# One attention stage and a state-space scan: mask, summed states and sums of squares taken from other places

## The reference

```
# attention 1: 16 query heads, 4 key heads, 128 wide, causal
qkv = x @ w_qkv.T
q, k = layernorm(q) * g + b, layernorm(k) * g + b      # per head, over its 128 values
q, k = rope(q), rope(k)
scores = q @ k.T / sqrt(128);  scores = where(causal, -inf, scores)
out = softmax(scores) @ v @ w_o.T
# state-space layer 1: 256 channels, 16 states n, 4 batches
state[n] = state[n] * exp(delta * A[n]) + delta * u * B[n]     # along the positions
y = sum over n of state[n] * C[n]  + D * u
```

## Time and profile before

| | |
|---|---|
| median of 3 runs | 912.32 us |
| the profiled execution's own time | 913.75 us |
| its span, first to last instruction | 912.0 us |
| busy: PE, DVE, ACT, POOL | 767.7, 703.3, 445.6, 340.6 us |
| mean granted TensorE clock | 0.924 |

### The profile page before, as it was taken

How to read it: one execution, slowest core, us unless ns; L and a number is a source line. 1 busy time by engine, 2 the same in 40 slices (tenths; PEclk the granted TensorE clock), 3 DMA queues, 4 the chain that set the end, 5 groups by cost and what they waited for, 6 DMA issues and landing times.

```text
span 912.0 us, 12288 instructions
## 1 busy us (share of the span) xinstructions
PE 767.7 (84%) x3984; PEld 563.1 (62%) x3984; DVE 703.3 (77%) x1229; ACT 445.6 (49%) x928; POOL 340.6 (37%) x242
## 2 busy tenths in 40 slices
PE   6771459877798996799999999999955799999997
PEld 2241346554433563477767776777743689999996
DVE  4869779889857976999999999999977544444443
ACT  1663368650336402666566556756642354444442
POOL 1001346552330422233333323432343286666663
PEclk9785579998799998999999999999987899999999
DMA  4313223345020212011111211111300243334431
GB/s 171 121 47 114 93 94 125 115 139 218 1 98 0 74 43 92 19 40 44 51 36 36 69 36 36 55 39 36 118 0 1 79 158 138 138 138 138 141 135 46
DMA packets 28884, 74.63 MB, mean 82 GB/s; under 512 B 3633, under 2 KB 6337, under 8 KB 28449
## 3 DMA queue, kind: packets, MB, share of 16 engines
q1 hardware_dynamic: 28384, 71.51, 23.2%
q10 hardware_dynamic: 448, 2.49, 0.8%
HBM read 72.55 MB, written 1.44 MB: 81 GB/s over the span
## 4 chain that ended last, share of the span: by engine, by line
PE 50%; DVE 26%; issue 11%; ACT 9%; POOL 3%; DMA 1%; POOLq 0%; DVEq 0%; SPq 0%; ACTq 0%
PE ps L1671 6%; PE ps L1785 6%; PE ps L1786 6%; PE ps L1787 6%; PE ps L1631 4%; DVE hS L976 3%; PE ps L1651 3%; PE ps L1750 3%; PE ps L1435 2%; PE ps L1738 2%; DVE arena L1280 2%; DVE hS L1006 2%; DVE ps L968 2%; PE ps L1408 1%; PE ps L1720 1%
## 5 line engine op out<-in xcount | busy, mean ns | idle before, releaser
L403 POOL TENSOR_TENSOR hS<-hS,BCb 128x512 f32<-128x512 f32 x64 | 81.6, 1278 | 131.9 <-issue 66.7
L1387 DVE SCALAR_TENSOR_TENSOR arena<-ps,arena 128x1024 f32<-128x1024 f32 x32 | 39.2, 1224 | 102.2 <-ACT arena L842 93.1
L426 POOL TENSOR_TENSOR hS<-hS,BCb 128x1024 f32<-128x1024 f32 x23 | 56.1, 2440 | 111.3 <-DVE ps L968 96.3
L1671 PE MATMUL ps<-WB,hT 128*128 128x512 f32 x192 | 88.0, 603 | 3.0 <-DVE arena L1261 2.0
L476 POOL TENSOR_TENSOR MHl<-arena,MHh 128x1024 fp32r<-128x1024 f32 x34 | 81.7, 2404 | 16.9 <-ACT MHh L845 16.9
L1416 PE MATMUL ps<-ident,hS 128*128 128x128 f32 x256 | 40.1, 311 | 54.7 <-POOL hS L426 31.2
L1785 PE MATMUL ps<-Wh,MHh 128*128 128x256 f32 x272 | 77.8, 286 | 6.0 <-POOL MHl L476 6.0
L1006 DVE TENSOR_TENSOR_SCAN hS<-dA,ps 128x512 f32<-128x512 f32 x64 | 78.1, 1220 | 2.2
L1786 PE MATMUL ps<-Wl,MHh 128*128 128x256 f32 x272 | 77.6, 285 | 0.0
L1787 PE MATMUL ps<-Wh,MHl 128*128 128x256 f32 x272 | 77.5, 285 | 0.0
L1416 PEld LDWEIGHTS ps<-ident,hS 128*128 128x128 f32 x256 | 32.6, 159 | 65.1 <-POOL hS L426 38.2
(11 more groups left out here) (233 smaller groups left out, 1967.4 us busy)
## 6 DMA issues: line engine op xcount, KB each, us to landing
BCb<-bc_dram SPq DMA_DIRECT2D x32, 512.0 KB, 3.7
BCb<-bcq_dram SPq DMA_DIRECT2D x64, 256.0 KB, 3.1
arena<-gate_dram SPq DMA_DIRECT2D x32, 512.0 KB, 3.7
WB<-in_we SPq DMA_DIRECT2D x34, 256.0 KB, 2.7
WB<-in_wqkv SPq DMA_DIRECT2D x1, 3072.0 KB, 12.7
WA<-in_wo ACTq DMA_DIRECT2D x1, 2048.0 KB, 7.7
WA<-in_ffn SPq DMA_DIRECT2D x1, 1408.0 KB, 7.9
pkb<-in_pk SPq DMA_DIRECT2D x2, 698.0 KB, 4.7
```

What stands on the lines that cost most here:

```text
L403: gp.tensor_tensor(h, h, qbc(q)[:, 1:2, :].broadcast_to([P, DT, S]), ALU.mult).then_inc(s["c_ready"], 1)
L426: gp.tensor_tensor(h, h, BCb[g % SB_LOADS][:, 1:2, :].broadcast_to([P, DT, HALF]), ALU.mult).then_inc(s["c_ready"], 1)
L1671: last = mm(ps[:, bank + t, :], hT[:, c, P * (2 * b + t):P * (2 * b + t) + P], WB[:, c, c0:c0 + 512], start=(c == 0), stop=(c == HC - 1))
```

## The change

1. `s1` writes the mask only to the two diagonal blocks, 2 x 128 columns in place of 384.
2. `times_cq` of every odd step is followed on GpSimd by an addition of the even step's product, also 128 x 512, behind a wait for the product's own semaphore; `accq` is issued for odd steps only, so PE has half the transposes. The counts that the others wait for follow (`cq_count`, the ring's waits in `scanq` and `yq_copy`).
3. `job_sum` goes from VectorE. `job_sq` is eight ACTIVATEs of 128 x 128, one for each head and half of the positions, and each also gives the sum of its row through `accum_out`. GpSimd's part of the job waits for `job_sq`.
4. In the plan's table the price of "sum" goes, so steps of the scan move to other slots.

```diff
@@ -265,6 +265,7 @@
+        cq_count = lambda q: LAYER_STEPS + 3 * (q // 2) + q % 2 + 1
@@ -321,7 +322,7 @@
...
             def load_bq(q):
...
-                sp.wait_ge(s["c_ready"], LAYER_STEPS + max(q - QRING + 1, 0))
+                sp.wait_ge(s["c_ready"], cq_count(q - QRING) if q >= QRING else LAYER_STEPS)
@@ -401,6 +402,9 @@
...
             def times_cq(q):
...
+                if q % 2:
+                    pool.wait_ge(s["c_ready"], cq_count(q))
+                    gp.tensor_tensor(h, h, qring(hS, q - 1), ALU.add).then_inc(s["c_ready"], 1)
@@ -454,7 +458,7 @@
...
             def job(j):
...
-                pool.wait_ge(s["job_sum"], j + 1)
+                pool.wait_ge(s["job_sq"], j + 1)
@@ -607,7 +611,7 @@
...
             def yq_copy(b):
...
-                act.wait_ge(s["acc_mm"], LAYER_STEPS + DS * (b + 1))
+                act.wait_ge(s["acc_mm"], LAYER_STEPS + DS // 2 * (b + 1))
@@ -751,10 +755,13 @@
...
             def job_sq(j):
...
-                if j:
-                    act.wait_ge(s["job_sum"], j)
+                if j >= 2:
+                    act.wait_ge(s["job_rope"], 8 * (j - 1))
-                sc.activation(job_s(j), ps[:, k:k + 2, :], ACT.Square).then_inc(s["job_sq"], 1)
+                for x in range(2 * REP1):
+                    c = slice(D1 * (x % REP1), D1 * (x % REP1) + D1)
+                    last = sc.activation(job_s(j)[:, x // REP1, c], ps[:, k + x // REP1, c], ACT.Square, accum_out=jst[:, j % 2, 0, x:x + 1])
+                last.then_inc(s["job_sq"], 1)
@@ -1001,7 +1008,7 @@
...
             def scanq(q):
...
-                dve.wait_ge(s["acc_mm"], LAYER_STEPS + max(q - QRING + 1, 0))
+                dve.wait_ge(s["acc_mm"], LAYER_STEPS + (max(q - QRING + 2, 0)) // 2)
@@ -1261,13 +1268,6 @@
-            def job_sum(b, i):
-                j = JOB[b, i]
-                if j >= 2:
-                    dve.wait_ge(s["job_rope"], 8 * (j - 1))
-                dve.wait_ge(s["job_sq"], j + 1)
-                v.tensor_reduce(jst[:, j % 2, 0, :], job_s(j).rearrange("p t (h d) -> p (t h) d", d=D1), AX.X, ALU.add).then_inc(s["job_sum"], 1)
-
@@ -1301,8 +1301,6 @@
-                elif kind == "sum":
-                    job_sum(*a)
@@ -1439,12 +1437,12 @@
...
             def accq(q):
...
-                if n == 0:
+                if n == 1:
-                pe.wait_ge(s["c_ready"], LAYER_STEPS + q + 1)
+                pe.wait_ge(s["c_ready"], cq_count(q) + 1)
@@ -1619,7 +1617,7 @@
-            step = iter(range(Q_IN_FFN))
+            step = iter(range(1, Q_IN_FFN, 2))
@@ -1639,7 +1637,6 @@
-                    accq(next(step))
@@ -1654,7 +1651,7 @@
-            for k in range(4):
+            for k in range(2):
@@ -1715,7 +1712,8 @@
...
             def s1(u):
...
-                mm(ps[:, 2 + p, 0:3 * P], identb[:], mask1[:], start=True, stop=True, skip_group_check=True)
+                diagonal = lambda z: z.rearrange("p (k n) -> p k n", k=3)[:, 0::2, :]
+                mm(diagonal(ps[:, 2 + p, 0:3 * P]), identb[:], diagonal(mask1[:]), start=True, stop=True, skip_group_check=True)
@@ -1905,7 +1903,7 @@
-    cost = {"rot": 2.6, "sum": 1.2, "rope": 3.2, "step": 2.0}
+    cost = {"rot": 2.6, "rope": 3.2, "step": 2.0}
@@ -1956,7 +1954,8 @@
-                    behind.append(("acc", q))
+                    if q % 2:
+                        behind.append(("acc", q))
```

## The result

The changed kernel takes 936.74 us (median of 4 runs, 936.55 to 939.52) against 913.01 for the kernel before in the same series (4 runs, 912.07 to 916.04): ratio 1.0261, 95% interval 1.023 to 1.0293, so 23.7 us slower. The forecast was 929.5 with a range of 908 to 945. The profiled execution took 936.63, its span is 934.8, and the clock's mean is 0.925 as before.

A forecast was written before the change was run, and what follows sets the result against it. Although PE and VectorE are nine tenths busy, the prediction took ScalarE's chain to set every loop step. Terms 12.0 - 1.3 + 1.5 + 1.0 + 1.3 + 2.9 - 0.2 = +17.2 on 912.3 gave 929.5 us, range 908 to 945.

The forecast's parts named there:

- the stall: In attention 1's loops, eight squares delay ScalarE's copy of the weights, so PE waits ahead of `pv`: 1.0 us a loop.
- The pieces and the walked loop: ScalarE's eight squares at 0.26 us take 2.08; followed through one loop, the next Square comes at 15.04, not 14.04.
- Rival (a): Each of ScalarE's eight squares costs the full 0.35 us, +12, 941 us; chance 0.17.
- The rest of the intervals: Between Squares, beyond the plain 12.0: VectorE-bound loops -1.3, three with a values' projection +1.5, plan's moves +1.3 us.
- the copy's term: On ScalarE, `yq_copy` of batch 1 moves ahead of six `da` and the squares: +3.3 us, with minus 2 against it.
- The start: Ahead of 385 us, three jobs with idle engines and the feed-forward part: -0.2 us.
- The last job and behind it: The last job's longer loop adds 1.0 us; five additions on GpSimd and the stage's end add 2.9.
- rival (d): TensorE's clock falls in each loop because PE stands idle: some 1.3 us a loop, +20, 950 us; chance 0.07.
- (b): Eight squares pass nearly as fast as one, so PE's and VectorE's lost work pays: loop 13.3, 901 us; chance 0.15.
- (c): VectorE was the true bound in more loops, so gain and stall cancel: 912 us; chance 0.05.
- PE's busy time: Half the accumulations and a third of the mask go from PE: busy time down by some 15 us.
- the collision: GpSimd's addition holds up VectorE's division, up to 1.2 us a pair: absorbed by slack in loops, +2.5 behind the last job.

The follow-up runs named there:

- e3_sq: Kernel before with only the eight squares with accumulators in place of the one Square and VectorE's reduction: 931.34 us, ratio 1.0206.
- e1_mask: Kernel before with only the mask written to the two diagonal blocks: 913.17 us, ratio 1.0002.
- e13_price: Whole change, but the plan's table keeps its old price of "sum", 1.2: 934.19 us, ratio 1.0225.
- e2_pair: Kernel before with only the products of two states summed on GpSimd and half the accumulations on PE: 940.65 us, ratio 1.0311.
- e6_nosum: Kernel before with its one Square, VectorE's reduction taken away and a constant for the sums: 907.01 us, ratio 0.9933.
- e12_change_halves: Whole change with four squares ahead of the probabilities' copy and four behind, VectorE's products bank by bank: 926.72 us, ratio 1.014.
- e8_beside_rot: Kernel before with pairs from step 10 on, added beside VectorE's products from PSUM while jobs last, PE taking them a slot later: 921.0 us, ratio 1.008.
- e11_loops_only: Kernel before with mask, squares in halves, VectorE's products bank by bank, and pairs only for steps 10 to 49, beside products from PSUM: 906.96 us, ratio 0.992.

## Why the prediction was right, and where its sum was not

The direction, the stall and the range held; the sum was +17.2 and the span grew by 22.8. A second cause, the additions beside VectorE, was priced at too little, and part of the nearness of the sum is luck, as told below.

- **The pieces and the walked loop.** 0.26 a piece was predicted; the starts lie 0.25 apart, so the copy comes at 2.02 and not at 2.08. `pv` follows it by 0.58 and not by 0.53: the two misses cancel, and `pv` stands at 2.60 where 2.61 was predicted. The rest of the loop (3.83, 4.89, 6.52, 11.40, 15.04) is each within 0.01. The 0.09 taken off the exponential's price for a piece comes from no row; the runs bear it out. Rival (a) at 0.35 a piece is out. e3_sq shows that the stall comes from the squares alone.
- **The rest of the intervals.** The 15 intervals grew by 17.2 us together; predicted were 12.0 - 1.3 + 1.5 + 1.3 = 13.5. Where VectorE was the bound, the loops of 14.28, 14.10 and 14.28 became 15.04: the reduction's going pays 0.07 to 0.25 in each as I had it, but in three loops and not five; in others the growth is 1.89, 1.24 and 1.30, above the 1.0. The two with a values' projection and no moved copy grew by 1.05 and 0.89, not by 0.5: PE's saved accumulations go into waits, as the mask's do in e1_mask. The third grew by 4.2, of which 3.3 was the copy's term, right in place and in size; e13_price takes it away again. But the 2.0 that was set against it, for a net of +1.3, is not there in the loops as a whole: by e13_price the plan's moves cost 5.4 us in the loops and win 2.9 behind them, net about +2.5.
- **The start, -0.2 predicted.** This step failed. The first job's squares are 3.56 us late (342.13 against 338.57) and those of the fifth job, still 0.94 (386.32 against 385.38); four jobs stand ahead of it, not three. GpSimd's additions hold VectorE up in the feed-forward part already: the `dbq` in the second line is 1.66 us and not 0.70.

```profile
311.80 1.26 POOL L407 TENSOR_TENSOR hS<-hS 128x512 f32<-128x512 f32 x1
311.96 1.66 DVE L1004 TENSOR_TENSOR ps<-DU,BCb 128x512 f32<-128x512 f32 x1
```

- **The last job and behind it**, +3.9 predicted: 294.8 - 290.1 = +4.7. This agreement is luck in part. Where the plan's steps stay in their slots, the rest grows by 7.6 (e13_price) and 7.7 (e2_pair). Seven additions stand there and not five, and seven divisions are held up, one of them as before; the moved steps hide 2.9 us of it.
- **Clock, rival (d).** Not in each loop: the granted clock is 1.00 in the one shown. But once, where the moved copy (`yq_copy` of the scan's batch 1) is followed by the squares and `pv` waits for 4.39 us: the mean over that loop is 0.89, the lower of the two levels (1.2 and not 2.4 GHz) for a part of it, and the product takes 1.22 us, not 0.70. The loop grew by 1.09, little more than the others.

```profile
528.04 1.22 PE L1736 MATMUL ps<-arena 128*128 128x256 f32 x2 [4.39 <-ACT arena L798]
```

```profile
525.47:541.65 16.18, 13.29 (x58) 9.59 (x59) 11.82 (x27) 8.52 (x40) 4.17 (x4) 0.89 0.05 17
```

- **Rivals (b) and (c).** Out by the loop of 15.04. What (c) said of VectorE, that it was the bound, is out by e6_nosum, but for 0.8 us. Two slips in the working change nothing: eight pieces at 0.35 are 2.80 and not 2.84, and (b)'s loop of 13.3 is 13.2 by its own terms.
- **PE's busy time.** It was to fall by some 15 us and fell by 8.3. In e2_pair, with half the accumulations gone, it did not fall at all (768.0 against 767.7). Why was not followed up.
- **The weight given to the two causes.** The prediction put almost the whole sum on ScalarE, and held the collision to be worth 2.5 us behind the last job and nothing in the loops, because it "falls into DVE's new slack". As a sum that was nearly right. As an account of what is wrong with the change it misled: by e2_pair the additions alone cost 28.0 us, 14.0 of them in the loops, and with the stall mended (e12_change_halves) 13 of the 23.7 us remain, some 2.5 of them the price's. The slack is there only while PE stands still for ScalarE: in e2_pair's loop of 15.14 us VectorE is busy for 14.93. The collision was priced from the one row of 1.36 us in the earlier trace rows; what was not asked is how often the addition would land on a division. In e2_pair's loop it does so by construction: GpSimd's product (404.08) starts with VectorE's scan (403.98) and takes about as long (1.27 and 1.22 us), the divisions stand behind the scan, and the addition behind the product (405.43), on top of them.

The Trainium skill ("SBUF — State Buffer", Who interferes with whom) says that VectorE in a two-port mode, which `tensor_scalar` can enter, and GpSimd lock each other out for the whole instruction, that whoever issues second is blocked, that a VectorE instruction with two SBUF inputs contends with a GpSimd instruction that reads SBUF, and that one with at most one SBUF input outside the two-port modes does not contend. The traces agree: 1.36 us for the division, 1.66 for `dbq` (two SBUF inputs), and 0.413 unchanged for a product with one input from PSUM. They also show the other order, GpSimd second: an addition that starts 0.12 us behind a `dbq` takes 1.70 us (438.24 in the changed kernel) and leaves the `dbq` at 0.70. With that rule the collisions could have been looked for, addition by addition, in the order of the two queues.

What stays open: the start. Its 3.56 us at the first job are tied to the additions by the rows above and by two runs on the kernel before: e2_pair, with additions in the feed-forward part, has that job's squares at 342.68, e8_beside_rot, without them there, at 336.83. Yet no run took them out of the feed-forward part alone in the whole change; and why the plain loops of e12_change_halves differ, 13.54 to 16.51, was not followed one by one.

## What to carry to other kernels

Ask of a piece of work on a chain not how long its engine is busy but who stands behind it in that queue: eight short pieces ahead of a copy cost 24 us, the same pieces split around it, with VectorE's products following bank by bank, about 3. Two costs that each lengthen the same loop don't add; mend one and the other appears, so run each edit alone before the sum is read. When work goes to GpSimd, ask which VectorE instruction it will lie beside: in this kernel the additions cost nothing that shows beside products with one input from PSUM, and up to about 1 us of VectorE each beside a division.

## What the runs showed of the hardware that was not expected

- A Square of 128 columns with its accumulator costs 0.25 us of ScalarE's queue, though its ACTIVATE (0.28) and read (0.19 to 0.25) sum to more: they overlap. Eight are 2.0 us where one Square of 1024 columns holds the next instruction for 0.92.
- GpSimd's addition of two 128 x 512 tiles takes 1.27 us beside VectorE's products from PSUM (e11_loops_only), as long as the product with a broadcast operand. Its mean of 1.36 in the changed kernel (1363 ns, 32 times) comes from the additions that are held up themselves, up to 1.71 us; the median is 1.28.
- The held VectorE instruction ends a fixed time after GpSimd's, by its shape: the division of 128 x 256 0.15 us after it (405.43 + 1.28 = 406.71, 405.50 + 1.36 = 406.86), the division of 128 x 128 0.08, `dbq` 0.56 (311.80 + 1.26 = 313.06, 311.96 + 1.66 = 313.62).
